# A fused Perceiver block on one core: first chunk and tail put in another order, six weight pieces' low parts made by GpSimd

## What is computed

```python
x = x + cross_attention(layernorm(x), ctx)      # x 64x512, ctx 6272x512, 32 query heads, 8 key/value heads of 128
    # q = (ln(x) @ Wq + bq); k, v = split(ctx @ Wkv + bkv); softmax(q k^T / sqrt(128)) @ v; @ Wo + bo
x = x + nf4_lora_mlp(layernorm(x))
    # each weight W = NF4[codes] * scales (blocks of 64), each product x W^T + (x A) B^T, rank 16
    # q,k,v -> a = (q+k+v)/3 -> o;  x1 = x + o;  h = silu(g(x1)) * u(x1);  x1 + down(h)
x = x + layernorm(x) @ W_base^T + b_base + 0.5 * irfft(sum over experts of masked decoder outputs)
```

## Time and profile before

| | us |
|---|---|
| median of 3 runs | 1040.94 |
| lowest and highest | 1040.31, 1045.56 |
| the profiled execution, its own time | 1042.83 |
| its span, first to last instruction | 1041.0 |
| TensorE busy in the span | 1017.1 (98%) |
| VectorE, ScalarE, GpSimd busy | 758.6, 591.5, 475.9 |

### The profile page before, as it was taken

How to read it: one execution, slowest core, us unless ns; L and a number is a source line. 1 busy time by engine, 2 the same in 40 slices (tenths; PEclk the granted TensorE clock), 3 DMA queues, 4 the chain that set the end, 5 groups by cost and what they waited for, 6 DMA issues and landing times.

```text
span 1041.0 us, 19685 instructions
## 1 busy us (share of the span) xinstructions
PE 1017.1 (98%) x7083; PEld 934.7 (90%) x7083; DVE 758.6 (73%) x1676; ACT 591.5 (57%) x1249; POOL 475.9 (46%) x639
## 2 busy tenths in 40 slices
PE   7989999999999999999999999999999999999997
PEld 5879889999999999999999999899999999999743
DVE  5767777767777687767876687677876687767756
ACT  5456566556756566555665566555756566555431
POOL 2344544455544545355544545444545534444340
PEclk9999999999999999999999999999999999999999
DMA  9841221222212222121211222211222214443994
GB/s 309 249 125 55 65 60 46 64 69 60 69 41 69 75 64 65 46 68 56 73 57 55 71 64 64 64 56 50 70 59 69 71 41 130 157 153 88 284 341 131
DMA packets 73473, 98.91 MB, mean 95 GB/s; under 512 B 8688, under 2 KB 42496, under 8 KB 73376
## 3 DMA queue, kind: packets, MB, share of 16 engines
q1 hardware_dynamic: 72288, 95.86, 30.1%
q10 hardware_dynamic: 896, 1.51, 0.4%
q0 software_dynamic: 192, 0.29, 0.1%
HBM read 82.81 MB, written 14.81 MB: 94 GB/s over the span
## 4 chain that ended last, share of the span: by engine, by line
PE 85%; DVE 5%; DMA 4%; ACT 3%; POOL 2%; issue 1%; ACTq 0%; POOLq 0%; DVEq 0%
PE p_kv L73 18%; PE p_kv L74 18%; PE p_kv L75 18%; PE p_t L675 7%; PE p_o L73 4%; PE p_o L74 4%; PE p_o L75 4%; PE p_s L73 2%; PE p_s L74 2%; PE p_s L75 2%; PE p_s L758 2%; DMA ctx_st<-in_ctx_t 1%; DVE slots L1298 1%; PE p_o L685 1%; DMA expanded_weights<-slots 1%; PE p_ot L663 1%
## 5 line engine op out<-in xcount | busy, mean ns | idle before, releaser
L521 POOL TENSOR_SCALAR slots<-code 128x512 f32<-128x512 bf16 x232 | 155.1, 668 | 223.8 <-DVE slots L1302 155.2
L1298 DVE TENSOR_TENSOR slots<-slots 128x512 f32<-128x512 f32 x232 | 176.5, 761 | 3.0 <-POOL slots L521 1.2
L541 POOL TENSOR_TENSOR slots<-slots 128x512 f32<-128x512 f32 x58 | 74.9, 1292 | 202.4 <-DVE slots L1298 202.4
L1107 ACT ACTIVATE slots<-code,drop_and_offsets 128x512 f32<-128x512 bf16 x232 | 148.8, 715 | 29.1 <-POOL slots L541 29.1
L1251 DVE TENSOR_TENSOR v_lo<-p_kv,v_hi 128x256 fp32r<-128x256 f32 x196 | 83.2, 424 | 107.7 <-ACT v_hi L1072 106.8
L1072 ACT ACTIVATE v_hi<-p_kv 128x256 fp32r<-128x256 f32 x196 | 75.4, 385 | 136.0 <-PE p_kv L75 135.1
L1263 DVE TENSOR_TENSOR pt_lo<-p_t,pt_hi 128x512 fp32r<-128x512 f32 x224 | 133.4, 617 | 25.5 <-ACT pt_hi L1083 25.5
L1253 DVE SCALAR_TENSOR_TENSOR k_lo<-p_kv,bk_sb,k_hi 128x448 fp32r<-128x448 f32 x112 | 76.3, 682 | 100.3 <-ACT k_hi L1072 99.3
L1072 ACT ACTIVATE k_hi<-p_kv,bk_sb 128x448 fp32r<-128x448 f32 x112 | 71.1, 635 | 130.8 <-PE p_kv L75 129.8
L1083 ACT ACTIVATE pt_hi<-p_t 128x512 fp32r<-128x512 f32 x224 | 115.1, 543 | 41.7 <-PE p_t L675 41.6
L73 PE MATMUL p_kv<-wkv_hi,ctx_even_hi 128*128 128x256 f32 x448 | 126.4, 282 | 1.1 <-DVE v_lo L1251 1.0
(11 more groups left out here) (239 smaller groups left out, 2696.1 us busy)
## 6 DMA issues: line engine op xcount, KB each, us to landing
code<-in_codes SPq DMA_DIRECT2D x58, 256.0 KB, 2.6
scale<-in_scales SPq DMA_DIRECT2D x114, 128.0 KB, 3.1
expanded_weights<-slots SPq DMA_DIRECT2D x56, 256.0 KB, 2.1
ctx_st<-in_ctx_t SPq DMA_DIRECT2D x96, 112.0 KB, 2.0
ring_hi<-expanded_weights SPq DMA_DIRECT2D x22, 256.0 KB, 5.7
ring_lo<-expanded_weights SPq DMA_DIRECT2D x22, 256.0 KB, 6.0
wq_hi<-in_wq SPq DMA_DIRECT2D x4, 1024.0 KB, 6.9
wq_lo<-in_wq SPq DMA_DIRECT2D x4, 1024.0 KB, 8.0
```

The costliest lines, as they stand in the source:

```text
L521: nc.gpsimd.tensor_scalar(slots[:, slot, :], code16[:], LINES[j][0], LINES[j][1], ALU.mult, ALU.add).then_inc(pool_lines, 1)
L1107: nc.scalar.activation(slots[:, slot, :], code16[:], ACT.Identity, bias=offsets[:, k:k + 1], scale=LINES[j][0]).then_inc(act_lines, 1)
L1298: nc.vector.tensor_tensor(slots[:, slot, :], slots[:, slot, :], slots[:, other, :], ALU.max).then_inc(merged, 1)
```

## The change

Four sets of edits. All rows about VectorE's or GpSimd's work on `wkv_lo` refer to the first.

1. The low parts of pieces 2 to 7 are made by GpSimd (`split_wkv_late`), in each of blocks 0 to 5 between its row-sum addition and its join of the tile. TensorE waits for a semaphore of their own.
2. The start: seven instead of three matmuls on cleared data ahead of the first product; context parts 0 and 3 are rounded and split in halves; no query work stands between the first key products, and query group 1 is projected before the first scores; the later groups move up (group 5 from block 1 to block 0), and so do the loads of Wq parts 5 and 7 in SyncE's queue.
3. In the blocks: ScalarE rounds the first context piece of a pair one value step later (all chunks), and in the first chunk's even blocks it computes its weight-tile lines before it rounds the third context piece.
4. The tail: the folding is cut into four parts placed one by one; the rank-16 product of o is written to four partition groups and added through four copies of `lb_o`, which GpSimd clears first; VectorE's merges of the last tile stand behind the first and second gate step, not in front of the first.

```diff
-                  (lb_o[:], lora_b[3 * RANK:4 * RANK, 0:HID])]
...
+        smalls += [(lb_o[32 * i:32 * i + RANK, :], lora_b[3 * RANK:4 * RANK, 0:HID]) for i in range(4)]
...
+        FIRST_PARTS = ((0, 0, 1), (0, 1, 1), (1, 0, 2), (2, 0, 2), (3, 0, 1), (3, 1, 1))
+        FIRST_DONE = ((1, 2), (3, 3), (4, 4), (5, 6))
@@ SyncE @@
                     if start:
+                        load_wq(5)
                         load_wkv(4)
                         load_wkv(5)
-                        load_wq(5)
...
+                    if start:
+                        load_wq(7)
                     load(2)
...
                         load_wkv(7)
-                        load_wq(7)
...
+                        sp.wait_ge(step("lb_o_cleared"), 1)
                         for dst, src in smalls:
@@ GpSimd @@
+            def split_wkv_late(w):
+                wait_apart(pool, wkv_rounded, w + 1, pool_passed)
+                nc.gpsimd.tensor_tensor(wkv_piece(wkv_lo, w), wkv_piece(wkv_raw, w), wkv_piece(wkv_hi, w).bitcast(F32),
+                                        ALU.subtract).then_inc(wkv_split_late, 1)
...
                     add_rowsum(n, 2 * pair)
+                    if s == 0 and 2 * pair + 2 < NKV:
+                        split_wkv_late(2 * pair + 2)
                     join(n)
...
                     add_rowsum(n + 1, 2 * pair + 1)
+                    if s == 0 and 2 * pair + 3 < NKV:
+                        split_wkv_late(2 * pair + 3)
                     if end:
+                        wait_apart(pool, kv_psum, k_use(NCH - 1, NKV - 2, 1) + 1, pool_passed)
+                        nc.gpsimd.memset(lb_o[:], 0.0).then_inc(step("lb_o_cleared"), 1)
@@ TensorE, start @@
-            for _ in range(3):
+            for _ in range(7):
...
             pe.wait_ge(wkv_split, 1)
             for k in range(KT):
-                if k == KT - 1:
-                    query_turn(0)
-                pe.wait_ge(first_split, k + 1)
                 for c in range(2):
+                    pe.wait_ge(first_split, FIRST_DONE[k][c])
                     project_keys(k_bank(NKV - 1, c), 0, 0, c, k)
-                if k == 1:
-                    query_product(0)
+            query_product(0)
+            query_turn(0)
+            query_product(1)
@@ TensorE, blocks 0 and 1 @@
                 turn_probs(i, 0, first)
+                if i == 0:
+                    query_product(5)
                 if not first:
                     turn_output(i - 1)
                 if i == 1:
-                    query_product(5)
+                    query_turn(5)
+                    query_product(6)
@@ ScalarE @@
-                        if t == 1:
+                        if t == 2:
                             round_ctx(s, h, half, 0, last)
...
+                if s == 0 and h % 2 == 0:
+                    lines(i + 1)
+                    round_ctx(s, h, half, 2, last)
+                    return
@@ VectorE, blocks @@
-                        if s == 0 and t == 4 and h + 2 < NKV:
-                            split_wkv(h + 2)
                 else:
                     for k in range(4):
                         merge(i, k)
-                        if s == 0 and k == 1 and h + 2 < NKV:
-                            split_wkv(h + 2)
@@ VectorE, tail @@
-            for k in range(4):
-                merge(NB + 1, k)
...
                 if c == 0:
+                    for k in range(4):
+                        merge(NB + 1, k)
+                else:
+                    gated_t(c - 1)
+                if c == 1:
                     merge(NB + 1, 4)
                     merge(NB + 1, 5)
-                else:
-                    gated_t(c - 1)
@@ TensorE, tail @@
-            def fold(n):
+            def fold(k):
...
             fold(0)
             project_out(7)
+            fold(1)
             pe.wait_ge(step("two_idents"), 1)
             mean_and_turn(0, xa)
-            fold(1).then_inc(w_used, len(FOUR))
+            fold(2)
...
             turn(av, pb[TURN_BANK])
+            fold(3).then_inc(w_used, len(FOUR))
...
-            into_rank(pb[RANK_BANK][0:RANK, 0:TOK], [la[:, k, 3 * RANK:4 * RANK] for k in range(KT)], ats, "low_o")
+            for k in range(KT):
+                m = nc.tensor.matmul(pb[RANK_BANK][32 * k:32 * k + RANK, 0:TOK], la[:, k, 3 * RANK:4 * RANK], ats[k],
+                                     start=True, stop=True)
+            m.then_inc(step("low_o"), 1)
...
-            add_low_rank(wo_psum, e_small[:, 0], lb_o[:]).then_inc(step("o_psum_t"), 1)
+            add_low_rank(wo_psum, e_o[:], lb_o[:]).then_inc(step("o_psum_t"), 1)
```

More of the change, by code:

```diff
@@ L712, in values @@
             def values(s, h, half, queries={}):
-                if s == 0:
-                    pe.wait_ge(wkv_split, h + 2)
+                if s == 0 and h == 0:
+                    pe.wait_ge(wkv_split, 2)
+                elif s == 0:
+                    pe.wait_ge(wkv_split_late, h)
                 for t in range(CT):
@@ L735, in prev_values @@
                 pe.wait_ge(kv_split, 2 + KV_USES * pair + CT)
-                if not static_first(i):
+                if static_first(i):
+                    pe.wait_ge(q_out, 6)
+                else:
                     pe.wait_ge(o_out, i)
@@ L842, in block_work @@
                 if i == 0:
-                    values(s, h, half, {0: ((query_product, 1),), 2: ((query_turn, 1), (query_product, 2)),
-                                        4: ((query_turn, 2),), 5: ((query_product, 3),)})
+                    values(s, h, half, {0: ((query_turn, 1),), 2: ((query_product, 2),), 4: ((query_turn, 2),),
+                                        5: ((query_product, 3),)})
                     query_turn(3)
@@ L913, in _ @@
                 block_work(NCH - 1, h, 0, False, True)
-            def fold(n):
-                slot = FOUR[n]
+            def fold(k):
+                slot = FOUR[k // 2]
                 pe.wait_ge(w_in[slot % WB], 32 * (slot // WB + 1))
-                for j in range(2):
-                    k = 2 * n + j
-                    for i in range(2):
-                        m = nc.tensor.matmul(pb[DOWN_BANK][i * TOK:i * TOK + RR, 0:TW // 2], ws[:, k, :],
-                                             tile_of(slot, j)[:, i], start=(k == 0), stop=(k == KT - 1))
+                for i in range(2):
+                    m = nc.tensor.matmul(pb[DOWN_BANK][i * TOK:i * TOK + RR, 0:TW // 2], ws[:, k, :],
+                                         tile_of(slot, k % 2)[:, i], start=(k == 0), stop=(k == KT - 1))
                 return m
@@ L1202, in _ @@
             round_wkv(0)
-            for k in range(KT):
-                round_first(k)
+            for k, c, n in FIRST_PARTS:
+                round_first(k, c, n)
             act.wait_ge(offsets_ready, 1)
             nc.scalar.activation(alpha[:, 3, 0:1], offsets[:, 0:1], ACT.Exp)
-            round_wkv(1)
-            query_out(0)
             act.wait_ge(vecs_in, 48)
@@ L1408, in finish_query, with split_first @@
                 nc.vector.tensor_tensor(q_lo[:, h], q_f[:], q_hi[:, h].bitcast(F32), ALU.subtract).then_inc(q_split, 1)
-            def split_first(k):
-                dve.wait_ge(first_rounded, k + 1)
-                nc.vector.tensor_tensor(even_lo[:, k], ctx_raw[:, k], even_hi[:, k].bitcast(F32), ALU.subtract).then_inc(
-                    first_split, 1)
+            def split_first(part, k, c, n):
+                dve.wait_ge(first_rounded, part + 1)
+                keys = slice(c * HALF, (c + n) * HALF)
+                nc.vector.tensor_tensor(even_lo[:, k, keys], ctx_raw[:, k, keys], even_hi[:, k, keys].bitcast(F32),
+                                        ALU.subtract).then_inc(first_split, 1)
             def split_wkv(w):
@@ L1497, in _ @@
             split_wkv(0)
-            for k in range(KT):
-                split_first(k)
-            split_wkv(1)
+            for part, (k, c, n) in enumerate(FIRST_PARTS):
+                split_first(part, k, c, n)
             dve.wait_ge(vecs_in, 48)
-            finish_query(0)
             for c in range(2):
                 split_keys(c, k_bank(NKV - 1, c), 0, c)
+            finish_query(0)
+            split_wkv(1)
             dve.wait_ge(cleared, 1)
```

33 lines of the change are left out of this document (18 added, 15 removed).

## The result

| | before | after |
|---|---|---|
| median of 7 runs each, on one chip | 1040.42 us | 1033.09 us |
| lowest and highest | 1038.67, 1045.56 | 1032.36, 1034.59 |
| profiled execution, its span | 1042.83, 1041.0 | 1032.82, 1030.7 |

The ratio is 0.9932, 95% interval 0.9916 to 0.9949. The change makes the kernel 7.3 us faster by the medians and 10.0 us by the two profiled executions. The ratios in this document use all executions but two slow ones (1427.3 us of before, 3545.14 us of the kernel with both pieces in the even block), and they differ from quotients of the medians by up to 0.0014.

A forecast was written before the change was run, and what follows sets the result against it. TensorE is busy without a gap from 150 us, so only first chunk, tail and rare stalls can shrink. Terms 2.3 + 1.7 + 2.7 + 1.0 + 2.0 = 9.7 take 1042.83 to 1033.1, less 1.9 gives 1031.2 us; range 1027 to 1036.

The forecast's parts named there:

- the forecast's own: Whole kernel: the main case, 1029.5 to 1033 us, given a chance of 0.45.
- The median of the runs lies 1.9 under the profiled one; taken over: Whole kernel: before's 1.9 us offset between profiled execution and median carried over, turning 1033.1 into 1031.2 us.
- The start: Up to block 0's scores: they start at 20.65, 0.4 us earlier, with one more product of 1.9 done; gain 2.3 us.
- Blocks 0 and 1: First chunk's first two blocks: the 2.4 us Wq wait goes, less 0.7 for VectorE's lateness; gain 1.7 us.
- In block 1 query work covers it: Block 1: the 1.2 us TensorE stall expected in blocks 3 and 5 is hidden by query work.
- the hold: First chunk's blocks: GpSimd's 2.5 us piece blocks VectorE's merges for its whole length; stalls 1.2 us in blocks 3 and 5.
- Blocks 2 to 7: First chunk's later blocks: 5.1 us of excess goes, less 2.4 of stalls; gain 2.7 us, leaving 102.6.
- Without this all 5.1 us of excess could go: Blocks 2 to 7: relieving VectorE of its subtractions could remove the whole 5.1 us excess over the steady state.
- ScalarE's lines now go in front of its rounding, so nobody of the chain waits: Under blocks 0 and 1: a context piece arriving some 1 us later delays nobody; no separate gain assigned.
- the hold misses the merges: Rival, blocks 2 to 7: late pieces fall behind the last merges, 2.4 us more gained, 1028.8 us; chance 0.20.
- All chunks: After 150 us: rounding context one step later removes most of 1.6 us of v_lo waits; gain 1.0, bounds 0 and 1.6.
- The tail: Kernel's end: 1.5 us gate waits go, plus 0.2 from folding and 0.3 from rank product; gain 2.0, bounds 0 and 2.5.

The follow-up runs named there:

- the kernel with both pieces in the even block: Changed kernel with ScalarE's rounding and GpSimd's low part of the odd block's piece moved into the even block: 1032.94 us, ratio 0.9934.
- repeated run of before: The kernel before, unedited, profiled a second time: 1040.38 us.
- the move alone: Kernel before with one edit, GpSimd making the low parts of pieces 2 to 7 in front of its join: 1040.41 us, ratio 1.0012.
- the run of the lines alone: Kernel before with one edit, ScalarE's next-tile lines in front of its last context rounding in the first chunk's even blocks: 1040.53 us, ratio 0.9990.
- the run with the lines late: Changed kernel with ScalarE's lines put back behind its rounding of the last context piece in the first chunk's even blocks: 1040.52 us, ratio 1.000.
- the run with the merges first: Changed kernel with VectorE's four merges of the very last lines put back in front of the first gate step: 1034.30 us, ratio 0.9942.

## Why the prediction was right, and where it wasn't

**The total.** 1031.2 was predicted and 1033.09 measured, inside the range of 1027 to 1036 and a little above the forecast's own 1029.5 to 1033. The sum was near: 9.7 us predicted, 10.0 between the profiled executions. What failed is the step "The median of the runs lies 1.9 under the profiled one; taken over". After the change the profiled execution lies 0.3 under its median. The repeated run of before shows why: the first profiled one was long by waits for `v_lo` and Wq, and the change removes just these, so they were counted once in the sum and once in the offset. The clock belongs there too. Of 61 further executions of before, 33 kept a mean granted clock of 0.999 or more and have a median of 1039.12 us; the 28 at 0.998 or less, like both profiled ones, have 1041.5. All seven of the changed kernel are at 0.999 or more. So half clock is a loss that only some executions of before have, and the start's 2.3 was sized on one that had it.

Against the repeated execution the same five terms are 3.05 (start), -0.2 (blocks 0 and 1), 2.45 (blocks 2 to 7), 0.2 (steady part) and 2.4 (tail), together 7.9, near the 7.3 of the medians. So the start, blocks 2 to 7 and the tail stand against either execution; the 1.4 us found below for blocks 0 and 1 is luck of the execution it was read from, and so is the 2.0 for the steady part.

**The start** (2.3): 2.35, right in size. Scores start at 20.59 (20.65 predicted) with product 1 done. The clock at 12 to 15.3 is 1.00, as predicted, but not by the four warm-up matmuls. With three and an idle time of 1.32 us it stayed up as well. Of the 1.5 us by which that is shorter than before's 2.79, the halved part gave 0.5 (first key product at 10.62, not 11.11); the other 1.0 is a later start of the warm-up matmuls in that execution (7.75, not 6.75), which is chance.

**Blocks 0 and 1** (1.7): 1.4 us against the first profile. The two executions differ by 70.86 - 67.14 = 3.7 up to block 2, and the start has 2.35 of it (0.47 and a product of 1.9). Against the repeated one, whose wait for Wq was 1.4 us, nothing is gained. The wait for Wq is gone, as said. Not foreseen were 0.7 us in block 0, where score statistics stand behind VectorE's piece 1, and the size of VectorE's lateness in block 1: a wait of 1.06 us for query group 7. "In block 1 query work covers it" was wrong, for there the hold fell on that query work:

```profile
60.10 2.37 POOL L571 TENSOR_TENSOR wkv_lo<-wkv_raw,wkv_hi 128x1024 fp32r<-128x1024 f32 x1
...
60.60 2.02 DVE L1435 CAST q_hi<-q_f 128x256 fp32r<-128x256 f32 x1
...
69.89 0.29 DVE L1435 CAST q_hi<-q_f 128x256 fp32r<-128x256 f32 x1
```

These rows are of the changed kernel, GpSimd and VectorE: a cast of 0.29 us took 2.02 beside GpSimd's piece.

**Blocks 2 to 7** (2.7): 2.24 us, or 2.45 against the repeated run. The hold is the predicted one: pieces of 2.40 us (2.5), starting 9.7 us behind the block's first score (9.6), two waits of 0.97 us (1.2) behind the holds of blocks 3 and 5, in the first scores of blocks 4 and 6. Block 2 brought another 0.99, for score statistics behind query group 7. That the hold is the cause was tested: the waits for `k_lo` and the long merges went once the piece stood elsewhere (behind the join, or in the even block). The Trainium skill's "SBUF — State Buffer", section "Who interferes with whom", has this hold as its rule, and names casts too as able to take the shared ports; by the 2.02 us above the trace agrees.

The other half of the step is wrong. The prediction credited VectorE's relief ("Without this all 5.1 us of excess could go"), but with the move alone blocks 2 to 7 took 106.34 us, about 1 more than before. What the prediction gave no price is what carries this part. "ScalarE's lines now go in front of its rounding, so nobody of the chain waits" stood there as a remark. Taken out, it costs 7.4 us, everything that the change gains (some 5.7 as waits, 1.7 as half clock behind one of them). The context transfer that GpSimd's piece delays is in order in front of ScalarE's exponentials; the reordered lines fill that time. The rival "the hold misses the merges" expected 2.4 us more from pieces outside the hold. Moving them out of it gained nothing in two kernels (1033.92, and 1032.94 with blocks 2 to 7 at 103.03) until the transfer was free as well, and then 3.1 us by the order of one call (102.44 to 99.32).

**All chunks** (1.0): 2.0 between the two executions, but that is chance of the first. The steady part took 755.78, 753.96, 753.17 and 756.59 us in the four profiled executions with the old rounding step, mean 754.9, and 752.9 to 754.1 in ten with the new, mean 753.5. So some 1.3 us, within the bounds of 0 and 1.6, from four executions that differ by 3.4 among themselves. TensorE's waits for `v_lo` behind 150 us were 1.6, 0.4, 0.3 and 2.4 us in the four and at most 0.2 in those with the new step.

**The tail** (2.0): 2.3 us, 1.3 of it by the merges behind the gate step. The remaining 1.0 lies with the rank product (0.30 us for eight matmuls, 0.62 before) and the spread folding (the wait for `xa` 0.3 instead of 0.7), not taken apart further. SyncE's three more transfers made nobody late.

## What to carry to other kernels

An engine that takes over work sets transfers as well as data: follow what its later instructions free, which load starts by that, and who stands in order behind its landing. Here one such chain decided between 7 us and nothing, and moving an unrelated instruction in front of the wait paid for it. Put a two-input instruction that moves to GpSimd where VectorE reads PSUM: beside such reads the 2.4 us piece held nothing here, beside two merges it cost 0.97 us twice. Size a change on more than one profiled execution when the terms are single waits of a few us, and look at the granted clock behind each long wait before you put a difference down to the wait alone.

## What was unexpected

- The clock: with 2.67 to 2.81 us of idle time in front of the first key product the granted clock was 0.52 to 0.56 at 12 to 15.3 us (both profiles of before, and the run of the lines alone), the lower level of 1.2 GHz; with at most 1.32 us it was 1.00. In block 1 it fell to 0.50 behind waits of 2.20 and 2.35 us (the run with the lines late, the run of the move alone) and stayed at 1.00 behind one of 2.38 (before).
- Warm-up matmuls can be a burden, or help by being slow. In the profiled execution of the run with the merges first, the same row that took 3.29 us elsewhere took 5.15, at a recorded clock of 1.00, and the scores started at 22.60 instead of 20.6:

```profile
7.78 5.15 PE L914 MATMUL p_t<-acc 128*128 128x256 f32 x14 [0.52 <-DVE xt L1522]
```

  Why it was slow the records don't show. The 2.0 us later start fits the 2.3 us by which that execution (1036.59) lies above its median (1034.30). In the run of the move alone its three took 2.92 us instead of 1.56, also at a recorded clock of 1.00; there they left only 0.40 us idle in front of the first key product, the clock stayed up, and the scores started earliest of all, at 19.98. The profiled execution of that run thus had this luck at its start and the half clock in block 1.
